# Graph attention on one core: two slots of every tile without a question, later slots in nested questions, and diagonals signalled without drains

## The chip, the cores and the metric

The kernel runs on one core of one Trainium2 chip. The metric is the device time of one execution in microseconds (us); lower is better. The engines are named as in the profile: PE (TensorE), with PEld for its weight loads, DVE (VectorE), ACT (ScalarE), POOL (GpSimd), SP (SyncE, which issues most transfers here). A q behind the name, as in POOLq, means the engine's own instruction queue: branches, semaphore work, register loads.

## The reference, cut to what matters

```python
h = maximum(layernorm(x), 0)                        # 8192 x 256
e = leaky_relu(h @ a[:256] + (h @ a[256:]).T, 0.2)  # 8192 x 8192
U = softmax(where(adj > 0, e, -9e15), axis=1)       # adj: sparse, some neighbours in a row
prop_u = U @ h
rowsum = sum(U * 0.5 * U, axis=1)
coe = sigmoid(temp)
xi = h * rowsum[:, None]
feat = coe[2] * (prop_u - xi) + (1 - coe[2]) * (h + prop_u - xi)
feat = soft_threshold(feat, 1e-6)
pu = U @ feat
odd = feat - coe[3] * pu
even = pu + odd * rowsum[:, None]
odd = coe[0] * odd + (1 - coe[0]) * h0
out = x + coe[1] * even + (1 - coe[1]) * odd
```

`adj` has 1 on its diagonal, and elsewhere 1 with a probability that falls with both the row's and the column's number. So the first rows have many neighbours, and most rows have few. It is read as float32, 256 MB.

## The kernel before

The 8192 rows are 64 tiles of 128. Tile 0, whose rows have most neighbours, is computed as a dense one beside the rest. Tiles 1 to 63 are computed by lists of neighbours, in two passes, one for each product with U.

**First pass.** Each engine has its own loop over the tiles (`turns`, two tiles for each turn of the loop), with semaphores between them. For each tile SP loads the adjacency in two halves. ACT turns each half into signs (L309, 128x4096), TensorE folds them into 16 blocks of keys (L321), and DVE finds in these keys the columns of up to 24 neighbours of each row (L1085 to L1145 and on). DVE then counts. TensorE sums the counts over the tile's rows (L984, L985, in SUMS). D is the number of *slots*: in slot k, every row of the tile fetches its k-th neighbour. Further neighbours of all rows together are at most 128 and go into one *tail* in which each of 128 places belongs to whatever row needs it. D is the weighted count, by the weights SLOTW, of the sums that are over 128 (L1189). CTL holds D + 1 for each tile (L1190), and the engines read it into a register with `slots_of` (L623), which is four instructions of the queue. A `COMPARE_BRANCH` for each `If(slots > k + 1)` then decides on each slot. Slots 0 to 8 are asked for one by one, then in pairs to 16; SLOTW makes D even there.

POOL gathers each slot by an indirect DMA of 128 rows (L634), then the tail (L649). In the first pass the rows come from `haug_d` (h and its two scores) and land in G. With the scores, DVE and ACT make the softmax weights WS. ACT then makes for each slot a diagonal matrix of weights, DG[k] = ident times column k (L680), in two lots: the first KG = 4 slots, drain and signal `diag_begun` (L682), the others, drain and signal `diag_ready` (L684). TensorE waits for `diag_begun`, multiplies a zero matrix into the accumulator (L688, start of the sum), adds DG[k] x G[k] for the first lot (L689), then does the sums and half a fold of the next tiles, and only then waits for `diag_ready` and adds the other lot (L693) and the tail (L696). DVE makes `feat` from the sum, and SP stores it in `feat_d`. The lists and weights of every tile stay in memory (IDX, JT, WGT, with D in CTL), copied by ACT (L811 to L815). In the trace this pass ends at about 1090 us.

**Second pass, the ring** (L1572 on). Its tiles go round in RING = 4 buffers. DVE copies a tile's lists and weights to the ring (`stage`, L1757, signal `staged`) once the product three tiles back is done. POOL waits for `staged` alone, reads D, and gathers the slots (L634; for tiles 1 to 3 L1683, part of them already gathered at the end of the first pass, SOON) and the tail from `feat_d`. ACT waits for `staged` and for the product two tiles back (`prod2_ready`), reads D, and makes the diagonals. TensorE waits for `diag2_begun`, for the output of the tile two back in the same accumulator (`out_made`), and for the gathers; it multiplies the first lot, waits for `diag2_ready`, multiplies the others, adds the tile's share of row 0's product (`own`, L1713) and the tail, and signals `prod2_ready`. DVE makes the output (L1764, L1777). SP loads four kinds of rows for two tiles at a time (L1606 to L1609) and stores two tiles at a time.

The order on each engine is that of the program text; nothing is planned at run time but the questions on D. A tile whose lists don't fit is written into a dense part of the program; CTL then still holds its D.

## Time and profile before

| | |
|---|---|
| median of 3 runs | 1500.11 us (1496.91 to 1509.17) |
| the profiled execution | 1488.81 us, its span 1487.2 us |
| mean granted TensorE clock | 0.808 |
| busy share of the span | PE 64%, DVE 63%, ACT 58%, POOL 41% |
| DMA | 415.70 MB, 280 GB/s in the mean |

The span is the time from the first to the last instruction that the profiler saw. Busy shares are a mean over both passes. Idle time of an engine is put down to what released it: another engine's instruction, a DMA, "issue" when it waited for nothing that the profile shows, "remote" where the releaser isn't known. A row of windows gives the stretch, its length, the busy time of PE, PEld, DVE, ACT and POOL with the number of instructions, the granted TensorE clock as a share of full speed, the mean busy share of the DMA engines and GB/s. A matmul or weight load of float32 shows as two instructions.

### The profile page before, as it was taken

To read this page: it belongs to the slowest core of one execution; us is meant where nothing else is said; L and a number is where in the kernel's file an instruction comes from. 1 tells how busy PE (TensorE), PEld (TensorE's weight loads), DVE (VectorE), ACT (ScalarE), POOL (GpSimd) and SP (SyncE) were. 2 spreads that over 40 slices of the span, in tenths; PEclk is the share of its full clock that TensorE was granted. 3 is DMA by queue.
4 is the path that set the end of the run, shared out by engine and by line. 5 is a ranking of instruction groups with operands and counts; after the bars stand their busy time and mean duration, and the time that the engine had idled before them with its cause. 6 is when DMAs were issued, how large, how long until landed. Compare 5 with 4: busy or idle time off the path is not lost.

```text
span 1487.2 us, 27559 instructions
## 1 busy us (share of the span) xinstructions
PE 953.7 (64%) x3629; PEld 576.7 (39%) x3630; DVE 932.0 (63%) x5233; ACT 863.0 (58%) x1840; POOL 602.7 (41%) x649
## 2 busy tenths in 40 slices
PE   3545776776676767667777777764266456565665
PEld 2521254443443433333334433332145344343433
DVE  7756556776778878888888888877511222323433
ACT  4673677877788888888888888881222121111111
POOL 1004354443333323322222222215566676666664
PEclk9975689889889888997887787876568777877778
DMA  6989887999999999999999999952344454555665
GB/s 182 358 288 370 335 319 276 336 339 349 353 347 353 378 368 372 371 379 387 374 384 376 366 380 378 371 208 69 87 123 127 120 164 138 162 172 179 191 193 160
DMA packets 146214, 415.70 MB, mean 280 GB/s; under 512 B 29166, under 2 KB 109054, under 8 KB 129782
## 3 DMA queue, kind: packets, MB, share of 16 engines
q1 hardware_dynamic: 115868, 345.65, 62.8%
q0 software_dynamic: 30304, 69.62, 15.0%
q14 instruction: 31, 0.25, 0.1%
q8 instruction: 11, 0.18, 0.0%
HBM read 398.37 MB, written 33.90 MB: 291 GB/s over the span
## 4 chain that ended last, share of the span: by engine, by line
DVE 31%; issue 25%; PE 15%; DMA 6%; another core or an unknown queue 5%; POOL 5%; ACT 4%; POOLq 4%; DVEq 3%; ACTq 1%; SPq 0%
PE TP L321 4%; PE ACC L689 3%; POOL W L634 3%; DVE XHO L1068 2%; PE ACC L693 2%; DMA W<-feat_d,IDT 2%; PE MISC L989 2%; POOLq L623 2%; DMA R<-in_x_dram 1%; ACT SG L309 1%; DMA R<-sc_d 1%; POOL R L634 1%; DVEq L257 1%; DVE JK L1135 1%
## 5 line engine op out<-in xcount | busy, mean ns | idle before, releaser
L309 ACT ACTIVATE SG<-W,ABOVE 128x4096 bf16<-128x4096 f32 x126 | 467.0, 3706 | 77.4 <-DVE cnt L1051 46.9
L634 POOL DMA_INDIRECT R<-haug_d,IDS x230 | 229.8, 999 | 598.2 <-issue 583.0
L321 PE MATMUL TP<-SG,FOLD 128*128 128x512 bf16 x1008 | 304.3, 444 | 0.0
L680 ACT ACTIVATE DG<-ident,WSR 128x128 f32<-128x128 f32 x230 | 76.1, 391 | 338.2 <-remote 181.4
L1777 DVE SCALAR_TENSOR_TENSOR R<-ACC,SELF,R 128x256 f32<-128x256 f32 x63 | 30.5, 484 | 279.3 <-remote 184.1
L688 PE MATMUL ACC<-XHO,ZB 128*128 128x256 bf16 x126 | 40.5, 321 | 217.1 <-ACTq L682 78.5
L634 POOL DMA_INDIRECT W<-feat_d,IDR x140 | 141.4, 1010 | 73.3 <-issue 73.3
L689 PE MATMUL ACC<-R,DG 128*128 128x256 f32 x446 | 162.3, 515 | 1.5 <-issue 1.5
L321 PEld LDWEIGHTS TP<-SG,FOLD 128*128 128x128 bf16 x1008 | 114.6, 122 | 114.4 <-issue 54.5
L689 PEld LDWEIGHTS ACC<-R,DG 128*128 128x128 f32 x446 | 105.0, 252 | 21.6 <-issue 3.0
L688 PEld LDWEIGHTS ACC<-XHO,ZB 128*128 128x128 bf16 x126 | 12.7, 101 | 249.7 <-issue 124.1
L689 PE MATMUL ACC<-W,DG 128*128 128x256 f32 x274 | 95.8, 493 | 4.8 <-issue 4.7
L680 ACT ACTIVATE DG<-ident,WS 128x128 f32<-128x128 f32 x230 | 75.6, 391 | 29.5 <-issue 29.5
L649 POOL DMA_INDIRECT R<-haug_d,IDT x63 | 62.8, 997 | 38.1 <-issue 38.1
L689 PEld LDWEIGHTS ACC<-W,DG 128*128 128x128 f32 x274 | 61.0, 242 | 20.8 <-issue 11.1
L634 POOL DMA_INDIRECT R<-feat_d,IDR x52 | 53.2, 1024 | 29.6 <-issue 26.8
L952 PE MATMUL OWNB<-HTS,R 128*128 128x256 f32 x116 | 39.5, 422 | 36.4 <-issue 19.6
L1713 PE MATMUL MISC<-R 128*128 128x256 f32 x128 | 51.0, 488 | 16.1 <-issue 15.8
L984 PE MATMUL MISC<-RC,ONESB 128*128 128x18 bf16 x61 | 11.6, 190 | 72.9 <-DVE RC L1183 72.6
L649 POOL DMA_INDIRECT W<-feat_d,IDT x48 | 48.9, 1020 | 21.5 <-issue 19.0
L805 ACT ACTIVATE WS<-SCR,msm 128x25 f32<-128x25 f32 x63 | 19.9, 316 | 57.5 <-DVE msm L1110 42.8
L989 PEld LDWEIGHTS MISC<-ED,RE 128*128 128x128 f32 x122 | 25.3, 259 | 62.8 <-DVE RE L1200 62.8
(295 smaller groups left out, 2286.4 us busy)
## 6 DMA issues: line engine op xcount, KB each, us to landing
W<-in_adj_dram SPq DMA_DIRECT2D x128, 2048.0 KB, 13.3
haug_d<-R POOLq DMA_DIRECT2D x8, 1056.0 KB, 9.7
HTS<-haug_d SPq DMA_DIRECT2D x64, 132.0 KB
R<-in_x_dram SPq DMA_DIRECT2D x8, 1024.0 KB, 6.5
R<-feat_d SPq DMA_DIRECT2D x32, 256.0 KB
R<-in_x_dram SPq DMA_DIRECT2D x32, 256.0 KB
R<-in_L_gnn_h_dram SPq DMA_DIRECT2D x32, 256.0 KB
feat_d<-FTS SPq DMA_DIRECT2D x63, 128.0 KB
```

What stands on the lines that cost most here:

```text
L309: nc.scalar.activation(SG[:, u, half(h)], W2[:, u, half(h)], ACT.Sign, scale=2.0 ** 100, bias=ABOVE[:], accum_out=DEG[:, u, h:h + 1]).then ...
L321: nc.tensor.matmul(KP[u], FOLD[:, b], SG[:, u, b * FW:(b + 1) * FW], start=False, stop=False)
L623: return eng.value_load(CTL[0:1, bass.ds(t, 1), 0:1].rearrange("a b c -> a (b c)"), min_val=1, max_val=KS1)
L634: pool.indirect_dma_start(out=g[:, k, 0:w], out_offset=None, in_=table, in_offset=bass.IndirectOffsetOnAxis(ap=ids[:, k:k + 1], axis=0), * ...
L649: pool.indirect_dma_start(out=g[:, KR, 0:w], out_offset=None, in_=table, in_offset=bass.IndirectOffsetOnAxis(ap=idt, axis=0), **limit).the ...
L680: nc.scalar.mul(DG[:, u, k], ident[:], weights[:, k:k + 1])
L688: nc.tensor.matmul(ACCS[u], ZB[:], COLS[:, 0:F], start=True, stop=False)
L689: first_slots(pe, slots, lambda k: nc.tensor.matmul(ACCS[u], DG[:, u, k], g[:, k, 0:F], start=False, stop=False))
L952: nc.tensor.matmul(ACC0, PTB[:, w], HTS[:, uc, 0:F], start=False, stop=False)
L989: nc.tensor.matmul(SPR, RE[:, u], ED[:], start=True, stop=True).then_inc(spread, 1)
L1713: return nc.tensor.matmul(ACC3, PTR[:, v], FR[:, v], start=False, stop=False)
L1777: nc.vector.scalar_tensor_tensor(OR[:, v], ACCS[v % 2], S1A[:, bass.ds(t, 1)], TR[:, v % 2], ALU.mult, ALU.add).then_inc(out_made, 1)
```

## The change

1. KM = 2: slots 0 and 1 are taken by every tile. SLOTW counts them always, so that CTL holds at least 3, and D is at least 2. POOL, ACT and TensorE do slots 0 and 1 without a question.
2. The questions for further slots are nested (`chain`): slot k + 1 is asked for only inside the body of slot k, so that a tile leaves at the first question that fails. In the first pass this holds within the first lot (up to KG = 4) and, anew, within the second. In the ring all slots are one chain (for tiles 1 to 3 on POOL, two).
3. The zero matmul L688 is gone: slot 0's product starts the sum.
4. ACT's two drains are gone. It makes the diagonals of slots 2 and on first and those of 0 and 1 last, and the last diagonal itself carries the signal. In the first pass the signal for the second lot is on the copy behind it (WGT, L811). In the ring there is one signal, `diag2_ready`, for all of a tile's diagonals, and TensorE waits for it once, before its first product; tile 0 now makes two diagonals there and waits for them.

```diff
@@ -28,6 +28,7 @@
     KL = 16
     HEAD = 8
     KG = 4
+    KM = 2
     KC0 = KR + 2
     RING = 4
     S0 = 4
@@ -379,11 +380,12 @@
             nc.gpsimd.iota(OFFS[:].rearrange("one (g s) -> one g s", s=FW // P), pattern=[[0, NT * P // FW], [-P, FW // P]], base=FW - P, channel_multiplier=0).then_inc(tri_set, 1)
             pool.wait_ge(tri_set, 2)
             nc.gpsimd.memset(NEGD[:, 0:1], 2.0 ** 20)
-            nc.gpsimd.memset(SLOTW[:, 0:1], 0.0)
+            nc.gpsimd.memset(SLOTW[:, 0:1], float(KM))
+            nc.gpsimd.memset(SLOTW[:, 1:KM + 1], 0.0)
             late = SLOTW[:, KP2 + 1:KC - 1].rearrange("p (a b) -> p a b", b=2)
             nc.gpsimd.memset(late[:, :, 0], 2.0)
             nc.gpsimd.memset(late[:, :, 1], 0.0)
-            nc.gpsimd.memset(SLOTW[:, KC - 1:KC], float(2 - KC))
+            nc.gpsimd.memset(SLOTW[:, KC - 1:KC], float(2 + KM - KC))
             nc.gpsimd.affine_select(out=TRI[:], in_=TRI[:], compare_op=ALU.is_gt, fill=0.0, base=0,
                                     pattern=[[1, P]], channel_multiplier=-1)
             nc.gpsimd.iota(back[:], pattern=[[-1, NT]], base=NT, channel_multiplier=0, allow_small_or_imprecise_dtypes=True)
@@ -635,65 +637,34 @@
                                         in_offset=bass.IndirectOffsetOnAxis(ap=ids[:, k:k + 1], axis=0),
                                         **limit).then_inc(arrived, 16)
 
-            def one(k):
-                with pool.If(slots > k + 1):
-                    begin(k)
-
-            for k in range(KG):
-                one(k)
+            begin(0)
+            begin(1)
+            chain(pool, slots, begin, KM, KG)
             if others_free:
                 others_free()
-            other_slots(pool, slots, begin)
+            chain(pool, slots, begin, KG, KR)
 
         def gather_tail(pool, g, idt, table, w, arrived, **limit):
             pool.indirect_dma_start(out=g[:, KR, 0:w], out_offset=None, in_=table,
                                     in_offset=bass.IndirectOffsetOnAxis(ap=idt, axis=0),
                                     **limit).then_inc(arrived, 16)
 
-        def first_slots(eng, slots, do):
-
-            for k in range(KG):
+        def chain(eng, slots, do, k, stop):
+
+            if k < stop:
                 with eng.If(slots > k + 1):
                     do(k)
-
-        def other_slots(eng, slots, do):
-
-            def pairs(k):
-                with eng.If(slots > k + 1):
-                    do(k)
-                    do(k + 1)
-                    if k + 2 < KR:
-                        pairs(k + 2)
-
-            with eng.If(slots > KG + 1):
-                do(KG)
-                for i in range(KG + 1, KP2):
-                    with eng.If(slots > i + 1):
-                        do(i)
-                pairs(KP2)
-
-        def diagonals(act, t, u, weights, begun, done):
-
-            slots = slots_of(act, t)
-
-            def one(k):
-                nc.scalar.mul(DG[:, u, k], ident[:], weights[:, k:k + 1])
-            first_slots(act, slots, one)
-            act.drain().then_inc(begun, 1)
-            other_slots(act, slots, one)
-            act.drain().then_inc(done, 1)
-
-        def first_products(pe, slots, u, g):
-
-            nc.tensor.matmul(ACCS[u], ZB[:], COLS[:, 0:F], start=True, stop=False)
-            first_slots(pe, slots, lambda k: nc.tensor.matmul(ACCS[u], DG[:, u, k], g[:, k, 0:F], start=False, stop=False))
-
-        def other_products(pe, slots, u, g, rw, done, between=None):
-
-            other_slots(pe, slots, lambda k: nc.tensor.matmul(ACCS[u], DG[:, u, k], g[:, k, 0:F], start=False, stop=False))
-            if between:
-                between()
-            nc.tensor.matmul(ACCS[u], rw, g[:, KR, 0:F], start=False, stop=True).then_inc(done, 1)
+                    if k < KP2:
+                        chain(eng, slots, do, k + 1, stop)
+                    else:
+                        do(k + 1)
+                        chain(eng, slots, do, k + 2, stop)
+
+        def diagonal(u, weights, k):
+            return nc.scalar.mul(DG[:, u, k], ident[:], weights[:, k:k + 1])
+
+        def slot_product(u, g, k):
+            nc.tensor.matmul(ACCS[u], DG[:, u, k], g[:, k, 0:F], start=k == 0, stop=False)
 
         def first_sync(sp):
             prepare_sync(sp)
@@ -807,8 +778,12 @@
                 act.wait_ge(w_made, t + 1)
                 nc.scalar.activation(WQ[:], WS[:, u], ACT.Square, accum_out=msm[:, u, 3:4])
                 nc.scalar.copy(SW[:, bass.ds(t + 1, 1)], WS[:, u, K:K + 1]).then_inc(sums_ready, 1)
-                diagonals(act, t + 1, u, WS[:, u], diag_begun, diag_ready)
-                nc.scalar.copy(WGT[:, bass.ds(t + 1, 1)].rearrange("p a k -> p (a k)"), WS[:, u, 0:KR])
+                slots = slots_of(act, t + 1)
+                chain(act, slots, lambda k: diagonal(u, WS[:, u], k), KM, KG)
+                diagonal(u, WS[:, u], 0)
+                diagonal(u, WS[:, u], 1).then_inc(diag_begun, 1)
+                chain(act, slots, lambda k: diagonal(u, WS[:, u], k), KG, KR)
+                nc.scalar.copy(WGT[:, bass.ds(t + 1, 1)].rearrange("p a k -> p (a k)"), WS[:, u, 0:KR]).then_inc(diag_ready, 1)
                 nc.scalar.copy(IDX[:, bass.ds(t + 1, 1)].rearrange("p a k -> p (a k)"), IDS[:, u])
                 nc.scalar.copy(JT[:, bass.ds(t + 1, 1)], IDT[:, u:u + 1])
                 act.wait_ge(sums_ready, t + 1)
@@ -978,7 +953,9 @@
                     nc.tensor.matmul(SPW, RE[:, ub], WS[:, ub, 0:K], start=True, stop=True).then_inc(w_spread, 1)
                     slots = slots_of(pe, tb + 1)
                     pe.wait_ge(diag_begun, tb + 1)
-                    first_products(pe, slots, ub, G[:, ub])
+                    slot_product(ub, G[:, ub], 0)
+                    slot_product(ub, G[:, ub], 1)
+                    chain(pe, slots, lambda k: slot_product(ub, G[:, ub], k), KM, KG)
                 if live(0):
                     pe.wait_ge(counts_ready, t + 1)
                     nc.tensor.matmul(SUMS[:, 0:KC], ONESB[:], RC[:], start=True, stop=True)
@@ -994,7 +971,8 @@
                 if live(2):
                     pe.wait_ge(diag_ready, tb + 1)
                     pe.wait_ge(rw_ready, tb + 1)
-                    other_products(pe, slots, ub, G[:, ub], RW[:, ub], prod_ready)
+                    chain(pe, slots, lambda k: slot_product(ub, G[:, ub], k), KG, KR)
+                    nc.tensor.matmul(ACCS[ub], RW[:, ub], G[:, ub, KR, 0:F], start=False, stop=True).then_inc(prod_ready, 1)
             pe.sem_inc(prod_ready, 2)
             for u in range(NH):
                 pe.wait_ge(h_done[u], uses(u))
@@ -1572,7 +1550,6 @@
         t2_loaded = [sem(f"t2_loaded{h}") for h in range(RING // 2)]
         staged = sem("staged")
         gathered2 = [sem(f"gathered2{v}") for v in range(RING)]
-        diag2_begun = sem("diag2_begun")
         diag2_ready = sem("diag2_ready")
         prod2_ready = sem("prod2_ready")
         s4_step = sem("s4_step")
@@ -1666,7 +1643,9 @@
             def body(t, r, v, live):
                 act.wait_ge(staged, t + 1)
                 act.wait_ge(prod2_ready, t - 1 + RING)
-                diagonals(act, t, v % 2, WSR[:, v], diag2_begun, diag2_ready)
+                chain(act, slots_of(act, t), lambda k: diagonal(v % 2, WSR[:, v], k), KM, KR)
+                diagonal(v % 2, WSR[:, v], 0)
+                diagonal(v % 2, WSR[:, v], 1).then_inc(diag2_ready, 1)
             ring_turns(act, body, 0, 0)
 
         def second_gpsimd(pool):
@@ -1687,13 +1666,11 @@
 
             def other_gathers(t):
                 slots = slots_of(pool, t)
-                for k in range(S0):
-                    with pool.If(slots > k + 1):
-                        gather(t, k, gathered2[t])
-                for k in range(SOON[t], KR, 2):
-                    with pool.If(slots > k + 1):
-                        gather(t, k, gathered2[t])
-                        gather(t, k + 1, gathered2[t])
+                late = lambda k: gather(t, k, gathered2[t])
+                late(0)
+                late(1)
+                chain(pool, slots, late, KM, S0)
+                chain(pool, slots, late, SOON[t], KR)
 
             def dense(n):
                 pool.wait_ge(staged, RING)
@@ -1712,15 +1689,18 @@
                     pe.wait_ge(t2_loaded[v // 2], 64 * r + 64)
                     return nc.tensor.matmul(ACC3, PTR[:, v], FR[:, v], start=False, stop=False)
                 if isinstance(t, int) and t == 0:
+                    pe.wait_ge(diag2_ready, 1)
                     own().then_inc(prod2_ready, 1)
                     return
                 slots = slots_of(pe, t)
-                pe.wait_ge(diag2_begun, t + 1)
+                pe.wait_ge(diag2_ready, t + 1)
                 pe.wait_ge(out_made, t - 1 + RING)
                 pe.wait_ge(gathered2[v], pe.value_load(ARR[0:1, bass.ds(t, 1)], min_val=16, max_val=16 * KS1 * NT))
-                first_products(pe, slots, v % 2, RINGS[v])
-                pe.wait_ge(diag2_ready, t + 1)
-                other_products(pe, slots, v % 2, RINGS[v], RWR[:, v], prod2_ready, own)
+                slot_product(v % 2, RINGS[v], 0)
+                slot_product(v % 2, RINGS[v], 1)
+                chain(pe, slots, lambda k: slot_product(v % 2, RINGS[v], k), KM, KR)
+                own()
+                nc.tensor.matmul(ACCS[v % 2], RWR[:, v], RINGS[v][:, KR], start=False, stop=True).then_inc(prod2_ready, 1)
             def dense(n):
                 pe.wait_ge(acc2_free, n + 1)
                 nc.tensor.matmul(ACC2, zeros[:], a_row[:, 0:F], start=True, stop=False)
```

## Rows read from the trace of the kernel before

**Rows 1.** The page's 40 equal slices of the span, in tenths busy.

```profile
DVE  7756556776778878888888888877511222323433
...
POOL 1004354443333323322222222215566676666664
...
DMA  6989887999999999999999999952344454555665
```

**Rows 2.** POOL's timeline: start, us, what, [idle before <-releaser].

```profile
951.13 1.00 POOL L634 DMA_INDIRECT R<-haug_d,IDS  x1 [8.51 <-issue]
952.43 0.99 POOL L634 DMA_INDIRECT R<-haug_d,IDS  x1 [0.30 <-issue]
...
964.14 1.00 POOL L634 DMA_INDIRECT R<-haug_d,IDS  x1 [8.23 <-issue]
```

**Rows 3.** Windows: a stretch of the first pass, and the whole ring.

```profile
583.00:787.00 204.00, 146.18 (x611) 79.77 (x611) 171.19 (x1060) 172.08 (x352) 54.80 (x55) 0.86 0.99 377
1092.40:1477.60 385.20, 225.62 (x728) 158.02 (x727) 112.88 (x416) 66.83 (x200) 255.66 (x252) 0.77 0.53 159
```

**Rows 4.** PE's timeline in a tile of two slots.

```profile
709.67 0.28 PE L688 MATMUL ACC<-XHO,ZB 128*128 128x256 bf16 x1 [0.95 <-ACTq L682]
709.80 1.12 PE L689 MATMUL ACC<-R,DG 128*128 128x256 f32 x4
712.80 0.20 PE L984 MATMUL MISC<-RC,ONESB 128*128 128x18 bf16 x1 [1.88 <-DVE RC L1183]
```

**Rows 5.** Timeline of all engines in a tile of four slots.

```profile
427.06 1.28 ACT L680 ACTIVATE DG<-ident,WS 128x128 f32<-128x128 f32 x4 [0.42 <-issue]
...
428.41 0.28 PE L688 MATMUL ACC<-XHO,ZB 128*128 128x256 bf16 x1 [1.54 <-ACTq L682]
...
428.79 0.20 ACT L811 COPY WI<-WS 128x16 f32 x1 [0.46 <-issue]
```

**Rows 6.** DVE's waits, 180 to 379 us: total, times, longest.

```profile
DVE SCR L1076 <- PE MISC L968: 14.7, 5, 4.7
```

**Rows 7.** Lines one by one: count, ns min/median/max, starts; idle before.

```profile
L639 POOLq COMPARE_BRANCH  x492: 3/40/712, 114.3 to 1475.2; - x164
...
L656 ACTq COMPARE_BRANCH  x508: 7/40/888, 178.1 to 1479.2; - x170
L656 PEldq COMPARE_BRANCH  x504: 3/77/712, 179.6 to 1481.3; - x168
...
L668 PEldq COMPARE_BRANCH  x126: 4/202/714, 188.3 to 1481.6; - x126
...
L688 PE MATMUL ACC<-XHO,ZB x126: 269/283/421, 179.6 to 1480.7; 128*128 128x256 bf16 x126
...
  ACTq L682: 148.0, 112
```

**Rows 8.** The chain of waits kept to POOL: start, us, what.

```profile
1385.67 0.70 issue
1386.37 0.02 POOLq L668
...
1387.81 0.71 POOLq L1676
...
1389.46 0.04 POOLq L639
```

**Rows 9.** POOL's timeline at a late first gather and a late tail.

```profile
1390.29 1.00 POOL L634 DMA_INDIRECT W<-feat_d,IDR  x1 [2.29 <-issue]
...
1463.74 1.00 POOL L649 DMA_INDIRECT R<-feat_d,IDT  x1 [2.03 <-issue]
```

**Rows 10.** Timeline of all engines at the start of the ring.

```profile
1110.45 1.41 ACT L680 ACTIVATE DG<-ident,WSR 128x128 f32<-128x128 f32 x4 [25.54 <-remote]
...
1112.02 1.86 ACT L680 ACTIVATE DG<-ident,WSR 128x128 f32<-128x128 f32 x6 [0.17 <-issue]
...
1114.04 0.42 PE L688 MATMUL ACC<-XHO,ZB 128*128 128x256 bf16 x1
```


## Prediction, made before the change was run

> **What bounds the kernel now.** I read the page first [rows 1]: the 40 slices (37 us each) fall into two passes, and a share over the whole span would hide it. In the first DVE is at 7 to 8 tenths and the DMA engines at 9; in the last 13 slices DVE and ACT nearly rest and POOL is at 5 to 7. So every edit must be priced twice.
>
> In the first pass the Pool's own timeline [rows 2] shows a tile every 13.0 us with two slot gathers and one tail gather. Over the 63 tiles the slot gathers counted tile by tile in that timeline go from 16 at the front to 2, and no tile has fewer than two (about half have exactly two). That settles the first question: taking two slots without asking adds no gather, no diagonal and no product with this input. DVE is what the rest turns round there: it is busy 171.2 of 204.0 us in the middle stretch [rows 3], and TensorE waits for it, 1.88 us before the counts' sum of a two-slot tile [rows 4]. The gaps that are left in DVE are its own step waits and the short answers of TensorE.
>
> The second pass is a ring of four tiles. Between the first ring gather and the last one lie 385.2 us [rows 3], in which POOL is busy 255.7 us with 252 gathers, so that 129.5 us are idle. Back to back the gathers stand 0.30 us apart [rows 2], so 252 x 0.30 = 75.6 us of the idle time belong to issuing them and 53.9 us are stalls. The floor of this pass, with these gathers, is 331.3 us, and only the 53.9 us can be won.
>
> **The change, part by part.** *The zero matmul (L688).* 126 times 283 ns [rows 7], but it overlaps the loads behind it: in the two-slot tile it starts at 709.67 and the first product at 709.80 [rows 4], so it costs 0.13 us, about twice that at the half clock. In the first pass it goes where TensorE then waits 1.88 us: nothing. Only in the first tiles, where DVE waits for TensorE's moved rows (14.7 us in 5 times, [rows 6]), it is on the path: 5 x 0.13 to 0.28 = about 1 us.
>
> *ScalarE's two drains (L682, L684).* TensorE is said to wait for L682 148.0 us in 112 times [rows 7]. Most of that is the diagonals themselves: in a four-slot tile they run from 427.06 to 428.34 and TensorE starts at 428.41 [rows 5]. A signal on the last diagonal can only save part of the 0.07 us. What does go is ACT's pause after the diagonals, 0.46 us before L811 [rows 5]. It lets the second half's signs begin 0.46 us earlier, but ACT itself waits for DVE and DMA later in the tile; cover gone, it would cost up to 0.46 x 63 = 29 us, and the signs would have to be what DVE waits for, which the 0.99 share of busy DMA [rows 3] and DVE's near-continuous work speak against. I take 1 us, with 0 and 6 as the bounds for all of ACT in the first pass.
>
> *The second drain replaced by the weights' copy.* The signal for the later diagonals comes behind one more ACT copy, 0.20 us [rows 5]; TensorE asks for it only after half a fold, so it is free.
>
> *The branches.* A tile with D slots asked, on ACT, POOL and TensorE each, four times, then once more (L668), and for D from 5 to 8 four times beyond that. Now it asks D - 1 times in the second pass up to D = 8 (the last question is the one not taken): for D = 2 five questions become one, for D = 3 two, for D = 5 nine become four. In the first pass, which keeps the cut after four slots, five become two for D = 2. One question takes 40 ns on POOL and ACT and 77 ns on TensorE when the body follows; the late one that is jumped over on TensorE has a median of 202 ns [rows 7]. For a two-slot tile of the ring this is about 2 x 77 + 2 x 202 = 558 ns of TensorE's sequencer, 4 x 40 = 160 ns of POOL's and the same of ACT's. In ordinary time POOL's part is hidden: a gather is 1.3 us from start to start, and its question, move and issue take far less, as the gathers that follow at 0.30 us show [rows 2]. TensorE's part lies partly behind its matmuls.
>
> The Trainium skill (Advanced Engine Details and Errata, Control Flow Timing) gives a compare-and-branch about 108 ns; the traced instructions above are shorter on POOL and longer on TensorE where they jump. By its figure four questions fewer would be an estimated 0.43 us per tile and engine, and if nothing hid them 27 us per pass; the gathers at 0.30 us say that something does.
>
> *Where the questions are not hidden.* The 53.9 us of stalls are not spread evenly. Followed in the chain of waits kept to POOL [rows 8], the stretch before a late gather shows ordinary sequencer instructions about 0.7 us apart (pieces of 0.70, 0.02 and 0.71 us), where a question takes 0.04 us a little later. The queue of gathers that POOL has ahead runs dry and the next gather comes 1.5 to 3 us late: I count 23 such delays at a tile's first gather (41.9 us) and 8 before a tail (8.6 us) in the Pool timeline, of which one of each kind stands in [rows 9] (2.29 and 2.03 us of idle time with the usual 0.30 in it). In such a stretch the number of instructions counts, not their length. A two-slot tile costs POOL's sequencer 13 of them (one for the loop, four to read the count, five questions, three moves); four fewer is 4/13 = 31%. In pairs of 1.4 us four instructions are 2.8 us, more than one delay. So between 31% and all of a delay may go. TensorE and ACT lose instructions in the same stretches, which brings prod2_ready and the next diagonals forward too. I take 40% of 53.9, that is 22 us (bounds 0 and 54), nearer to the share of instructions because a stretch of slow instructions need not fall on the questions.
>
> *Diagonals waited for all at once.* TensorE in the ring waited for four diagonals and now waits for all. ACT makes a diagonal every 0.29 us (1.28 us for four, [rows 5]), and it may start only when the product two tiles back is done. For tile 3 its ten diagonals end at 1113.88, and TensorE comes to that tile at 1114.04 [rows 10]: free by 0.16 us. Bounds: 0, and 0.29 us for every diagonal beyond four in tiles 3 to 15, some 30 of them, 9 us. I take 0. Queued behind this wait on TensorE are the products of that tile alone.
>
> *Small things.* One memset more on POOL in the first us, two diagonals made for tile 0 that nobody uses (0.69 us of ACT before TensorE's first own-row product, which waits for loads): nothing.
>
> Sum: 1 + 1 + 22 = 24 us. The profiled execution took 1488.81 us (its span is 1487.2), so 1464.8, which is 0.984 of it. The median of the three timed runs is 1500.11, 0.8% above that execution, and the sum carries over as a ratio: 1476.
>
> **Rivals.** *A: the stalls stay.* The slow stretches last as long as they last whatever the engines want to issue (they come with the ring's loads); then POOL's floor and the 54 us both stay, and only the first pass's 2 us and at most a few of latency go: 1488.8 - 4 gives 1496. For it: at delays POOL is near the wait for the staged lists as well, and in this pass DVE waits long for releases that the profile can't name. Against it: within a slow stretch POOL's own instructions are visibly the slow thing.
>
> *B: the stalls nearly go.* The 2.8 us per tile cover a whole delay of 2 us. 54 + 2 us off: 1488.8 - 56 = 1432.8, or 1444. Against it: some delays come from products that are themselves long.
>
> *C: the wait for all diagonals decides.* ACT is released by the product two tiles back; where that release arrives late (ACT waited 25.54 us before tile 3's diagonals, [rows 10]) each diagonal past the fourth is now paid in full before the first product, 9 us, and if the same lateness reaches the two- and two-slot tiles, where the drains' signal came at about the same point, nothing comes back. With the gain of the branches absent, 1488.8 + 9 gives 1509. It decides once ACT begins a tile's diagonals less than 0.29 us x D before TensorE is free for it.
>
> *D: the slots differ from what the trace shows,* a tile with one slot that now has two: 1.3 us a piece on POOL. The counted gathers exclude it.
>
> **How the numbers follow.** Forecast 0.52 (8 to 35 us off in the profile, 1465 to 1492), A 0.34, B 0.07, C 0.06, D 0.01. The range leaves out B's end and C beyond its price: 1450 to 1509. The before runs span 0.8%, so 1% is about what can be told from no change. Faster by over 1% (under 1485): three quarters of the forecast's chance, and B, 0.50. Slower by over 1% needs C at double its price: 0.05. The rest, 0.45, is within 1%.
>
> **What would show it.** In the profile after: still no tile with fewer than two gathers and the same 192 + 60 ring gathers; first-pass tiles at 13.0 us; no L688 and no drain; TensorE's first product of a tile 0.13 us earlier behind its last diagonal; ring stretch 363 us, with 108 us of it idle on POOL instead of 130. If the ring stays near 385 us with the same number of late gathers, the step that fails is the 40%. If TensorE waits for ScalarE at the start of the ring's heavy tiles, C holds. If the first pass is shorter by more than 6 us, ACT's 0.46 us was on the path after all.

## The result, and the profile after

The changed kernel takes 1512.26 us in the median of 12 runs (1508.59 to 1516.38), the kernel before 1501.86 us in the median of 12 (1494.11 to 1509.17). The ratio is 1.007, 95% interval 1.0048 to 1.0092: slower by 0.7%, where I had forecast 1.6% faster, and 3 us above my range. The profiled execution took 1509.57 us, its span is 1508.0. The two traces stand further apart than the medians: the profiled execution of before took 1488.81 us, 13 us less than its median. What the change costs in time is therefore read from the medians, and the traces show where it arises.

The page's 40 slices, to hold against [rows 1]:

```profile
DVE  7755657767778888888888888875312213233443
...
POOL 1004354443332233322222222236556665656664
...
DMA  6989888988999999999999999922334445556554
```

The first pass looks as before. The stretch of the first pass and the ring, in the columns of [rows 3]:

```profile
583.00:787.00 204.00, 144.29 (x582) 78.80 (x597) 171.18 (x1064) 172.10 (x354) 52.86 (x53) 0.86 1.00 381
1087.70:1494.20 406.50, 205.24 (x662) 158.04 (x661) 111.20 (x413) 63.84 (x198) 254.24 (x252) 0.74 0.51 150
```

The ring, from the first gather of tile 4 to the end of the last gather, has grown from 385.2 to 406.5 us. POOL is busy for the same time with the same 252 gathers (254.2 us against 255.7), so its idle time has grown from 129.5 to 152.3 us. With 75.6 us of it for the usual 0.30 us between gathers, the stalls went from 54 to 77 us. They were to fall to 32.

They also have another form. Before, the gathers of the ring were late 29 times by more than 0.3 us (beyond the usual 0.30), twice by more than 3. Now they are late 17 times, always at a tile's first gather, 16 times by 4.1 to 5.6 us, and from tile 20 on once every four tiles. In between they follow each other 0.30 us apart. One such stop in the timeline of the changed kernel:

```profile
1410.26 0.59 PE L1703 MATMUL ACC<-W,R 128*128 128x256 f32 x2
...
1412.95 1.00 POOL L648 DMA_INDIRECT W<-feat_d,IDT  x1 [0.31 <-issue]
...
1416.01 0.48 DVE L1757 SCALAR_TENSOR_TENSOR R<-ACC,SELF,R 128x256 f32<-128x256 f32 x1 [9.08 <-remote]
...
1416.62 0.69 ACT L664 ACTIVATE DG<-ident,WSR 128x128 f32<-128x128 f32 x2 [10.53 <-remote]
...
1418.52 1.00 POOL L636 DMA_INDIRECT R<-feat_d,IDR  x1 [4.57 <-issue]
```

TensorE's last product of a tile (L1703) ends at 1410.85. DVE, idle for 9.08 us, takes its result only at 1416.01, and ACT, which needs the same signal, starts at 1416.62. The profile names no releaser ("remote"), since the one that it knows had long been done. POOL's last gather ended at 1413.95, and it had to wait for the lists that DVE stages behind that signal. The trace's records of the signals themselves say the same: those of this product and of the one before it, which ended 2.4 us apart by the records of TensorE, were raised 0.17 us apart, at 1415.81 and 1415.98. Until just before that the queues of POOL and SP run slow instructions, and the last slow one of each ends at 1415.74. The trace has 48 signals for 61 products of the ring, so some records are missing. Of these 48, 33 came 1.7 to 3.5 us after POOL had ended a row of back-to-back gathers, 12 during a row (seven of these in its first 6 us), 3 more than 7 us after the last gather. Only 9 of the 48 came within 0.5 us of the end of a product. The first tile shows the longest case:

```profile
1087.52 0.59 PE L1703 MATMUL ACC<-W,R 128*128 128x256 f32 x2
...
1100.73 1.00 POOL L648 DMA_INDIRECT R<-feat_d,IDT  x1 [0.30 <-issue]
...
1105.21 0.48 DVE L1757 SCALAR_TENSOR_TENSOR R<-ACC,SELF,R 128x256 f32<-128x256 f32 x1 [27.45 <-remote]
```

The product ended at 1088.11, POOL went on gathering until 1101.73, the signal was raised at 1105.00, and DVE started at 1105.21. The kernel before has the same: DVE waited 27.50 us there for "remote".

The transfers of this stretch, in the same columns as [rows 3]:

```profile
1410.00:1415.00 5.00, 0.85 (x4) 0.40 (x3) 0.00 (x0) 0.00 (x0) 3.03 (x4) 0.79 0.72 233
1415.00:1420.00 5.00, 1.81 (x4) 1.51 (x5) 3.71 (x14) 1.39 (x4) 1.17 (x2) 0.50 0.01 4
```

In the window of the stop the DMA engines run dry as well (0.01 of them busy), so no transfers go on behind it that would pay it back.

TensorE also waits longer for ACT in the ring: 95.8 us in 13 times, all before slot products, where the trace of before has 14.5 us in 4 times, before the zero matmul (L688). The page's group of slot products in the ring (busy, mean ns, idle before):

```profile
L667 PE MATMUL ACC<-W,DG 128*128 128x256 f32 x356 | 123.5, 500 | 169.5 <-ACT DG L664 95.8
```

The nested questions do what they should. ACT asked 508 times in L656 alone [rows 7], and once more for each tile in L668; now it asks 361 times in all:

```profile
L655 POOLq COMPARE_BRANCH  x385: 18/45/1392, 115.3 to 1488.4; - x193
L655 ACTq COMPARE_BRANCH  x361: 34/40/50, 179.4 to 1497.7; - x181
L655 PEldq COMPARE_BRANCH  x360: 65/77/360, 180.8 to 1500.5; - x180
```

### The profile page after: what moved, and what is told of

Its sections match the earlier page's. It is cut to its first block, busy times and chain, and to the rows that moved or that the text cites. A ratio compares the mean times of both kernels' runs of the same rounds, so it can differ in the third digit from the quotient of the medians.

```text
span 1508.0 us, 25842 instructions
## 1 busy us (share of the span) xinstructions
PE 918.6 (61%) x3440; PEld 571.2 (38%) x3504; DVE 931.4 (62%) x5233; ACT 852.2 (57%) x1842; POOL 602.1 (40%) x650
## 4 chain that ended last, share of the span: by engine, by line
DVE 31%; issue 24%; another core or an unknown queue 14%; PE 14%; ACT 7%; DMA 3%; DVEq 3%; ACTq 2%; POOLq 0%; POOL 0%; SPq 0%
PE ACC L667 5%; PE TP L322 3%; DVE XHO L1046 2%; ACT DG L664 2%; ACT SG L310 2%; PE MISC L966 1%; DMA R<-in_x_dram 1%; ACTq L625 1%; DVEq L258 1%; DVE JK L1113 1%; DVE E L1108 1%; ACT R L414 1%; DVE FOUND L1051 1%; DVE FOUND L1031 1%
## 5 line engine op out<-in xcount | busy, mean ns | idle before, releaser
L322 PE MATMUL TP<-SG,FOLD 128*128 128x512 bf16 x948 | 293.9, 451 | 4.9 <-issue 1.3
L667 PE MATMUL ACC<-R,DG 128*128 128x256 f32 x564 | 184.0, 474 | 115.2 <-ACT DG L664 67.8
L667 PE MATMUL ACC<-W,DG 128*128 128x256 f32 x356 | 123.5, 500 | 169.5 <-ACT DG L664 95.8
L667 PEld LDWEIGHTS ACC<-R,DG 128*128 128x128 f32 x564 | 123.0, 230 | 146.7 <-ACT DG L664 73.6
L667 PEld LDWEIGHTS ACC<-W,DG 128*128 128x128 f32 x356 | 87.9, 256 | 199.3 <-issue 172.5
L975 PE MATMUL ACC<-R,RW 128*128 128x256 f32 x126 | 48.9, 477 | 0.5 <-ACT RW L815 0.5
L961 PEld LDWEIGHTS MISC<-RC,ONESB 128*128 128x128 bf16 x61 | 6.3, 103 | 112.0 <-DVE RC L1161 110.3
```

Source lines behind the costliest of these rows:

```text
L322: nc.tensor.matmul(KP[u], FOLD[:, b], SG[:, u, b * FW:(b + 1) * FW], start=False, stop=False)
L667: nc.tensor.matmul(ACCS[u], DG[:, u, k], g[:, k, 0:F], start=k == 0, stop=False)
L975: nc.tensor.matmul(ACCS[ub], RW[:, ub], G[:, ub, KR, 0:F], start=False, stop=True).then_inc(prod_ready, 1)
```

## The experiments

Each kernel was timed in 5 rounds beside the kernel before on the same chip, which gave 6 to 12 times of it; each ratio is to the kernel before in these rounds. The ring and the stalls are read from POOL's timeline in each profiled execution. Stalls are what POOL's idle time from gather to gather has beyond 0.30 us each, so a pause put in counts as one. The last column is the number of gathers late by more than 3 us. A trace is one execution and need not be a typical one: that of e4 took 1499.85 us, 12 us less than the median of e4, and that of e12 1503.51, 10 us more. So the shorter ring of e4 and the longer one of e12 are not read as effects.

| run | what it is | ratio, 95% interval | ring us | stalls us | over 3 us |
|---|---|---|---|---|---|
| before | | 1 | 385.2 | 54 | 2 |
| after | the change | 1.007, 1.0048 to 1.0092 | 406.5 | 77 | 16 |
| e1 | change in the first pass alone | 0.9946, 0.9921 to 0.997 | 386.8 | 57 | 1 |
| e2 | change in the ring alone | 1.0132, 1.0103 to 1.0161 | 404.9 | 75 | 16 |
| e3 | change, early signal kept | 1.003, 0.9997 to 1.0062 | 394.7 | 66 | 9 |
| e4 | change, flat questions | 1.0073, 1.0045 to 1.0101 | 394.9 | 65 | 8 |
| e5 | e1, no zero product in the ring | 0.9968, 0.9939 to 0.9998 | 389.8 | 59 | 5 |
| e6 | e1 and POOL's part of the ring | 1.0084, 1.005 to 1.0119 | 406.4 | 78 | 17 |
| e7 | e1, TensorE waits for all diagonals | 1.0036, 1.001 to 1.0061 | 396.4 | 67 | 9 |
| e8 | change, zero product back | 1.0062, 1.0039 to 1.0085 | 402.8 | 72 | 16 |
| e9 | e6 and 4 idle questions | 0.9944, 0.9924 to 0.9963 | 393.7 | 63 | 5 |
| e10 | e1 and 4 idle questions | 0.9967, 0.9947 to 0.9988 | 392.6 | 63 | 1 |
| e11 | e6 without h0 loads | 1.0087, 1.0056 to 1.0118 | 411.5 | 83 | 17 |
| e12 | e1 without h0 loads | 0.9949, 0.9927 to 0.9972 | 399.2 | 69 | 8 |
| e13 | e6 and a pause of 0.54 us a tile | 1.0037, 1.0007 to 1.0066 | 403.4 | 74 | 11 |
| e14 | change and this pause | 1.0005, 0.998 to 1.0029 | 393.9 | 65 | 7 |
| e15 | e6 and a pause of 0.97 us a tile | 0.9953, 0.9928 to 0.9977 | 388.7 | 58 | 3 |
| e16 | e6, 0.97 us every second tile | 1.0043, 1.0015 to 1.0071 | 399.2 | 68 | 9 |
| e17 | e6 and a pause of 0.75 us a tile | 0.995, 0.9925 to 0.9975 | 394.5 | 64 | 6 |
| e18 | change and a pause of 0.97 us | 0.9908, 0.9874 to 0.9943 | 389.1 | 60 | 3 |

**Which pass.** e1 has the change in the first pass and the ring of before, e2 the other way round.

> The change in the first pass alone, the second pass (ring) as before. In the traces the last early gather of the first pass stands at 1059.1 us before and at 1054.0 after, and the ring takes 385.2 us before and 406.5 after. If the two passes add up (theory 1): the first pass is shorter by 5 us and the ring stays, 0.3% faster than before, ratio 0.995 to 0.998. If the end of the first pass decides in which rhythm the ring falls (theory 2): the ring is longer here too, ratio 1.005 or more.

> The change in the ring alone, the first pass as before (but the slot count with its new weights). Theory 1 (the ring's own edits cost): ratio 1.008 to 1.014, a first gather late by 4 to 5 us once in four tiles, as in the trace after. Theory 2 (the rhythm comes from where the first pass ends): the ring at 385 to 395 us, ratio 1.000.

The two add up: 0.9946 and 1.0132 give 1.008, measured 1.007. The first pass gains 8 us (4 to 12), the ring loses 20. Each ring also keeps its rhythm behind the other first pass: 1 gather late by over 3 us in e1, 16 in e2.

**Which edit of the ring.** e3 makes diagonals 0 and 1 first:

```diff
-                chain(act, slots_of(act, t), ..., KM, KR)
-                diagonal(v % 2, WSR[:, v], 0)
-                diagonal(v % 2, WSR[:, v], 1).then_inc(diag2_ready, 1)
+                diagonal(v % 2, WSR[:, v], 0)
+                diagonal(v % 2, WSR[:, v], 1).then_inc(diag2_begun, 1)
+                chain(act, slots, ..., KM, KR)
+                act.drain().then_inc(diag2_ready, 1)
```

> The changed kernel with the ring's early signal again: ACT makes diagonals 0 and 1 first and signals them with the second one, then the others, drains and signals; TensorE waits for the first signal before slot 0 and for the second before slot 2. If the wait for all diagonals costs (the prediction's rival C), the gain is in tiles 3 to 20, which have most slots: up to 9 us, ratio to before 0.999 to 1.001, and the first late gathers of the ring become fewer. If it doesn't, ratio 1.007 as the changed kernel, and the four-tile rhythm stays.

> The changed kernel, but in the ring ACT, POOL and TensorE ask as before for slots 2 and 3 one by one, then once for the rest: three questions for a tile of two slots, where the change has one. If the nested questions (fewer instructions, but a longer jump over all further slots) are what costs, the ring is back at 385 to 395 us, ratio 0.997 to 1.000. If they help as I forecast, it is slower than the changed kernel by some us: 1.008 to 1.012. If they are neither, 1.007.

The early signal gives back 0.4 points, between the two expected ratios and at the edge of what can be told: the intervals of e3 and of the change overlap. One or three questions make no difference to the time (e4). The next three start from e1, the better kernel, and add one edit of the ring each; e8 starts from the change.

```diff
 e5, first_products
-            nc.tensor.matmul(ACCS[u], ZB[:], COLS[:, 0:F], start=True, stop=False)
-            first_slots(..., start=False, stop=False))
+            first_slots(..., start=k == 0, stop=False))
 e7, second_tensor
                 pe.wait_ge(diag2_begun, t + 1)
+                pe.wait_ge(diag2_ready, t + 1)
```

> The kernel with the change in its first pass alone (ratio to before 0.9946), and in the ring one edit more: the zero matmul is gone, slot 0's product starts the sum, all else as before. The change's ring costs 1.3% in all, the early signal with its drain gives back 0.4 points of it, the flat questions none. If the zero matmul is part of the rest (theory Z: it let TensorE load and start ahead of the diagonals), ratio 1.000 to 1.005. If it is free, as I forecast, 0.993 to 0.996.

> The kernel with the change in its first pass alone, and in the ring POOL's part of the change alone: two gathers without a question, the others nested. If a faster POOL crowds the transfers (theory P: the gathers of a round run back to back against the loads, and the engines then stand until the transfers are done), the late gathers are fewer and 4 to 5 us each, ratio 1.000 to 1.006. If POOL's questions are neither here nor there, 0.993 to 0.996; if they help as I forecast, 0.985 or less.

> The kernel with the change in its first pass alone, and in the ring one edit more: TensorE waits for all diagonals of a tile (both signals, the drains kept) before its first product. If the single wait costs (rival C), 3 to 9 us more than 0.9946: ratio 0.997 to 1.001, and most of it in tiles 4 to 20, which have more than four slots. If not, 0.993 to 0.996.

> The changed kernel with the zero matmul back in the ring, ahead of slot 0, behind the same waits. Theory Z: ratio falls from 1.007 to about 1.000. If it is free: 1.006 to 1.009.

The zero product can't be told from free: e5 is 0.2 points above e1, e8 0.1 below the change. POOL's part alone costs 1.4 points, more than I had expected of it, and has the whole new rhythm. POOL's timeline in e6:

```profile
1408.88 1.00 POOL L636 DMA_INDIRECT W<-feat_d,IDR  x1 [0.30 <-issue]
1410.18 0.99 POOL L648 DMA_INDIRECT W<-feat_d,IDT  x1 [0.30 <-issue]
1415.68 0.99 POOL L636 DMA_INDIRECT R<-feat_d,IDR  x1 [4.50 <-issue]
```

The wait for all diagonals costs 0.9 points beside POOL's questions of before, but beyond e6 the whole change costs nothing more (1.007 against 1.0084): the two don't add up.

**Questions or transfers.** e9 and e10 put questions on POOL that are never true and gather nothing.

```diff
+        def idle(eng, slots):
+            with eng.If(slots > KS1 - 1):
+                eng.sem_inc(unused, 1)
 e9, POOL's gathers of the ring
             begin(0)
+            idle(pool, slots)
             begin(1)
+            idle(pool, slots)     (three times)
```

> The kernel with the change in its first pass and in POOL's part of the ring (ratio 1.0084), with four questions more on POOL in each tile of the ring's loop, whose answer is always no: one behind slot 0's gather, three behind slot 1's. They gather nothing and wait for nothing. Theory P (POOL's questions, slow in the slow stretches, hold its gathers back, and the other engines' signals come through in the gaps): POOL is as before, ratio back to 0.993 to 0.998, and the late gathers become more and shorter. The forecast's theory (each question costs in a slow stretch): 1.009 to 1.015. If neither holds: 1.008.

> The kernel with the change in its first pass alone (ratio 0.9946), with four questions more on POOL in each tile of the ring's loop, one ahead of each question for slots 0 to 3, whose answer is always no. Theory P: no slower, 0.990 to 0.997, since the ring stands for signals and not for POOL. The forecast's theory: eight slow instructions where there were four cost half of 22 us or more, 1.000 or above.

> The kernel with the change in its first pass and in POOL's part of the ring (1.0084), without the ring's loads of h0 after its first four tiles; the output is then computed with those four tiles' h0. It moves 0.25 MB less for each pair of tiles, 7.7 MB in all. If the stops last until the crowded transfers are through (theory P), each late first gather shrinks from 4.2 us by the share of the transfers, by a quarter or more, and the ratio falls by 0.5 points or more, to 1.003 or less. If the stops are a matter of the engines' instructions alone: 1.006 to 1.010, the late gathers still 4 us each.

> The kernel with the change in its first pass alone (0.9946), without the ring's loads of h0 after its first four tiles; the output is then computed with those four tiles' h0. Theory P: it gains as well, but less than the other, since POOL's pauses already let signals through: 0.985 to 0.993. If transfers have no part in it: 0.993 to 0.996.

Four useless questions make the kernel with POOL's new part 1.4 points faster. Put on top of the questions of before (e10), four more cost 0.2 points, within the noise, where the forecast's theory asked for 1.000 or above. The timeline of e9 has the gaps of before again, here before a tail:

```profile
1430.97 1.00 POOL L743 DMA_INDIRECT R<-feat_d,IDR  x1 [0.30 <-issue]
1432.27 1.00 POOL L743 DMA_INDIRECT R<-feat_d,IDR  x1 [0.30 <-issue]
1435.68 1.00 POOL L648 DMA_INDIRECT R<-feat_d,IDT  x1 [2.40 <-issue]
```

h0 is 256 of the 1152 KB that SP moves in the ring for each pair of tiles (feat, x, h0 and the output 256 KB each, the rows of tile 0's product 128). The two kernels leave most of its loads out, and compute another output for it. POOL's gathers, which move 23 MB beside SP's 32 in the changed kernel from 1100 to 1470 us, stay as they are. Leaving h0 out changes neither ratio (1.0087 against 1.0084, 0.9949 against 0.9946), and the trace of e11 still has 17 gathers late by over 3 us. So nothing speaks for stops that last until a crowd of SP's transfers is through; a crowd of POOL's own was not tried. What was left is theory G: the other engines' signals come through while POOL makes a gap between gathers, and slow questions are one way to make one.

**A gap without a question.** POOL writes a buffer that nobody reads behind each tail gather:

```diff
+                pool.wait_ge(paused, t)
                 pool.wait_ge(staged, t + 1)
 ...
                 gather_tail(pool, RINGS[v], ...)
+                nc.gpsimd.memset(IDLE[:, v], 0.0).then_inc(paused, 1)
```

> The kernel with the change in its first pass and in POOL's part of the ring (ratio 1.0084), with a memset of 128x512 bf16 on POOL (0.51 us, of a tile that nobody reads) behind each tile's tail gather in the ring. Theory G (other engines' signals come only in the first 5 us of a row of back-to-back gathers or about 2 us behind its end): the row is three gathers in a two-slot tile instead of twelve; if a gap of 0.9 us is enough, the 4 us stops are gone, the ring is 331 + 60 x 0.55 = 364 us and the ratio 0.980 to 0.988. If such a gap isn't enough for a signal, the pauses come on top of the stops: 1.008 to 1.03. Theory P (the slow questions themselves): a memset is no question, so 1.008 or more as well.

> The changed kernel whole (1.007), with the same memset of 0.51 us behind each tail gather of the ring. Theory G: 0.985 to 0.995, above the run beside it by what the wait for all diagonals costs (0.9 points where it was tried alone). If the pause doesn't let signals through: 1.007 to 1.03.

> As the first of these, with a memset of 128x1024 bf16, about 1.0 us, behind each tail gather. Theory G: if 0.51 us was enough, this costs 60 x 0.5 = 30 us more, ratio 2 points above it; if it wasn't, this one brings the gain: 0.99 to 1.00. Without G: 1.01 to 1.05.

> As the first of these, with the memset of about 1.0 us behind every second tail gather: the same time of pauses in all, rows of six gathers (7.8 us) in two-slot tiles. Theory G: signals still come within each row's first 5 us, so nearly as good as the run with a short pause in each tile, 0.983 to 0.995. If what counts is the pause in each tile: worse by a point.

The sign was right and the size wrong. 0.54 us takes 0.5 to 0.7 points off, but a stop of 2 to 5.5 us still comes every third to sixth tile. With 0.97 us the last stop comes at tile 14. The idle time behind a tail gather grows from 0.30 to 1.13 us by it, which is 49 us of pure delay in the ring on the engine that sets the floor, and yet the kernel gets 1.3 points faster: without the pauses the stalls of the trace are 10 us in e15, against 78 in e6 and 50 with the short pause of e13. The timeline of e15:

```profile
1404.80 0.59 PE L713 MATMUL ACC<-W,R 128*128 128x256 f32 x2
...
1405.49 0.97 POOL L1727 MEMSET IDLE<- 128x1024 bf16 x1
1405.61 0.48 DVE L1822 SCALAR_TENSOR_TENSOR R<-ACC,SELF,R 128x256 f32<-128x256 f32 x1 [0.58 <-PE ACC L713]
...
1406.13 0.69 ACT L697 ACTIVATE DG<-ident,WSR 128x128 f32<-128x128 f32 x2 [1.75 <-PE ACC L713]
...
1406.62 1.01 POOL L637 DMA_INDIRECT R<-feat_d,IDR  x1 [0.16 <-POOL IDLE L1727]
```

The product ends at 1405.39 and DVE has its result at 1405.61, ACT starts at 1406.13. DVE's waits from 1250 to 1480 us (total, times, longest), of the changed kernel:

```profile
DVE R L1757 <- remote: 109.1, 12, 13.2
DVE R L1757 <- PE ACC L1703: 25.4, 7, 7.6
```

and of e15:

```profile
DVE R L1822 <- PE ACC L713: 92.3, 24, 6.3
...
DVE R L1822 <- remote: 9.6, 2, 6.8
```

The waits without a known releaser fall from 109.1 us to 9.6, and most of what is left is named by the product itself. In the whole ring of e15, 27 of 48 recorded signals came within 0.5 us of a product's end, against 9 of 48 in the changed kernel. The windows of this stretch, after and in e15:

```profile
1250.00:1480.00 230.00, 118.51 (x364) 90.28 (x365) 79.10 (x294) 34.85 (x104) 140.12 (x138) 0.76 0.56 165
```

```profile
1250.00:1480.00 230.00, 135.50 (x427) 96.94 (x428) 95.18 (x305) 35.93 (x106) 191.19 (x192) 0.80 0.60 178
```

In the same 230 us the DMA engines move 178 GB/s instead of 165, and POOL's busy time has the memsets in it. DVE's 95.2 us against 79.1 are for the most part not more work: it runs 305 instructions instead of 294. Its copies take longer where they run into a memset of POOL:

```profile
1406.27 0.29 DVE L1805 COPY IDR<-WI 128x16 int32 x1
...
1414.31 1.68 DVE L1805 COPY IDR<-WI 128x16 int32 x1
...
1414.99 0.97 POOL L1727 MEMSET IDLE<- 128x1024 bf16 x1
```

In this stretch the copy of L1805 takes 0.95 us in the mean of the 16 times in which it overlaps a memset, and 0.21 us in the other 27. So the pause has a price on DVE too. Rows of six gathers are too long already (e16), so what I expected of it was wrong.

> The kernel with the change in its first pass and in POOL's part of the ring (1.0084), with a memset of 128x768 bf16 on POOL (about 0.75 us) behind each tail gather of the ring. With 0.51 us (1.0037) a stop of 2 to 4 us came every fourth tile all the same; with 0.97 us (0.9953) the trace has none from tile 18 on, only 0.8 us more than the usual 0.30 in each tile. If 0.75 us is enough as well: 0.57 us in each tile, 60 x 0.23 = 14 us less than the long pause, 0.986. If the limit lies above it: between the two others, 0.997 to 1.003, with a stop of 2 to 4 us every four to six tiles.

> The changed kernel whole (1.007) with the long pause of 0.97 us behind each tail gather of the ring. If held signals are all of the change's loss in the ring, the wait for all diagonals costs only where a signal is held, and this comes to the level of the same pause in the other kernel: 0.993 to 0.998. If the wait for all diagonals costs by itself, its 0.9 points stay: 1.002 to 1.006.

0.75 us does as well as 0.97 (0.995 and 0.9953): stops remain in its trace, every third to seventh tile up to tile 48. Without the pauses 28 us of stalls are left in it against 10 in e15, and the shorter pauses save 13. Most of its recorded signals are still late, only 11 of 49 within 0.5 us of a product's end. With the long pause the changed kernel comes to 1490.47 us against 1503.3 of before, 0.9908. That is the lowest ratio of all, though its interval meets that of e1 (0.9921 to 0.997), so that a gain over the change in the first pass alone isn't sure. It isn't slower than e15 (0.9953), so there the wait for all diagonals costs nothing that can be seen. So this edit too seems to cost only where signals are held.

## Why the prediction was wrong

- *Which input, which slots.* Right: 252 gathers in the ring, as before.
- *The zero matmul, 1 us.* In the ring, where I put it at nothing, right within what can be measured: e5 and e8 move by 0.2 and 0.1 points. In the first pass, where the 1 us is, it wasn't tried alone.
- *ACT and the first pass, 2 us in all.* The sign was right, the term too small: e1 gains 8 us (4 to 12). I had named over 6 us as the sign that ACT's pause of 0.46 us was on the path after all; the interval leaves that open, and which of the edits brings the gain wasn't tried apart. A tile of two slots takes 12.94 us in the trace after instead of 13.01 [rows 2] (first gathers at 946.20 and 959.14), which over 63 tiles is 4 us. But single traces carry little here: in the kernels with this same first pass and no pause the ring's first gather lies anywhere from 1083.5 to 1094.4 us.
- *The questions, 22 us of 54.* This is the step that failed. I took the slow sequencer instructions before a late gather for what made it late, costed four fewer at 40% of the stalls, and bounded the term by 0 and 54, a gain in either case. The stalls grew by 23 us. The slow questions were what made gaps between gathers in which the other engines' signals arrived. Taking them away made the rows longer, 12 to 14 gathers from tile 32 on where the trace of before has at most 11, and each stop there 4 to 5 us. e6 shows the loss on POOL's part alone, e9 takes it back by idle questions, e15 by a pause that asks nothing.
- *Rival C, the wait for all diagonals, 9 us.* On the ring of before it costs 0.9 points, 13 us (e7), more than its price, and I gave it a chance of 0.06 and priced it for tiles 3 to 15 only. Where it acts the single traces don't agree on: of the 10 us by which the stalls of e7 exceed those of e1, 9 are in tiles 4 to 33, while e3 gives back 8 of its 11 us in tiles 34 to 63, nearly all of two slots. That it stretches the path from a late signal to the next product would fit both, but isn't shown. In the whole change it isn't an addend: with POOL's part in place nothing is left of it. That C's sum, 1509 us, lies 3 us from the result is luck, for POOL's part alone makes the whole loss.
- *Rival A* had named the clue: in the ring DVE waits long for releases that the profile can't name. I used it as an argument about latency and did not ask when those releases came. In the trace of before, 27 of its 51 recorded signals of products came 0.5 to 2.8 us after POOL's last gather of a row.
- *The chances.* "Faster by over 1%" should be 0.46 by my own sum (three quarters of 0.52, and 0.07), not 0.50. It changes nothing in the account.

What stays open is the mechanism that holds the signals. Shown is when they come, and that gaps on POOL take the loss back, whether they are made of questions or of a memset of 0.75 us or more in each tile. With 0.97 us the signals come in time as well; with 0.75 us most still don't. The medians follow the traces (e6, e9, e15), but every timed execution on record comes with its span and its granted clock, so no run shows a kernel without the profiler's records. The Trainium skill (NOTIFIC — the notification-queue block, Interfaces) says that a full internal buffer of such records can stall an engine; no run here shows whether that plays a part in the ring.

## What to carry to other kernels

Before removing instructions from an engine that issues small gathers back to back, look at when the others' signals arrive: idle time with an unnamed releaser that ends just behind a row of gathers means that this engine's gaps are doing work. Then bound the edit on both sides of zero. A deliberate pause on such an engine is a cheap test (a memset and a wait for it, 1.6 points here), and the kernel with the lowest ratio has it together with the change.

## What the runs showed of the hardware

- Signals of TensorE's products came up to 17 us late while POOL issued indirect gathers 1.3 us apart. In the changed kernel 33 of 48 came 1.7 to 3.5 us after a row of 4 to 26 gathers. With a memset of 0.97 us between rows of three, the one shown let DVE start 0.22 us after its product's end, and 27 of 48 came within 0.5 us.
- In these stretches register and branch instructions of POOL and SP, in the kernel before of ACT and TensorE too, stand 0.7 us apart or take as long, where one takes 0.04 us otherwise, 0.08 on TensorE [rows 7, 8]. In the ring of before 53 of POOL's 357 compare-and-branches, 34 of ACT's 365 and 23 of TensorE's 369 took over 0.5 us; in that of the changed kernel 33 of POOL's 186 and none of ACT's and TensorE's.
- 22% less of what SP moves changed no ratio (e11, e12).
- A DVE copy that overlaps a POOL memset of 0.97 us took 0.95 us in the mean, 0.21 us otherwise (L1805 of e15, 1250 to 1480 us).
